# Square sums of the queries as four plain float32 matmuls in array strips, in a cross-attention and FFN kernel

## The reference

```python
q = (layernorm(x) @ Wq).reshape(B, Sq, H, D)      # 16 x 100 tokens, H = 16 heads, D = 128
k = (ctx @ Wk).reshape(B, Skv, H, D)              # 361 context rows of width 256 for each sequence
q = q * rsqrt(mean(q * q, over D) + 1e-5) * gq    # the same for k with gk
attn = softmax(q . k / sqrt(D))
x = x + (attn @ v) @ Wo
x = x + ffn(layernorm(x))                          # 512 -> 4096 gate and up, gelu(gate) * up -> 512
```

## Time and profile before

| | us |
|---|---|
| median of three runs | 1963.61 (1963.55 to 1963.71) |
| the profiled execution | 1964.14 |
| its span | 1962.3 |
| busy PE / DVE / POOL / ACT in the span | 1942.6 / 1598.0 / 1139.9 / 1008.1 |

### The profile page before, as it was taken

One profiled execution on the slowest core, in us unless ns is written; L12 is line 12 of the kernel. 1 busy time (PEld: TensorE's weight loads), 2 busy tenths in 40 slices (PEclk: granted clock), 3 DMA queues, 4 the chain that ended last, 5 costly groups with the idle time before them and its releaser, 6 DMA issues.

```text
span 1962.3 us, 33608 instructions
## 1 busy us (share of the span) xinstructions
PE 1942.6 (99%) x11232; PEld 1852.5 (94%) x11232; DVE 1598.0 (81%) x2995; ACT 1008.1 (51%) x2338; POOL 1139.9 (58%) x1272
## 2 busy tenths in 40 slices
PE   8999999999999999999999999999999999999999
PEld 7899899999999999999999999998999999999999
DVE  8878887787887787887778887888888888888875
ACT  5655555555555555555555553444444444444442
POOL 7765665423434333444333335888888888878871
PEclk9999999999999999999999999999999999999999
DMA  6444443423333334333233333211111111111101
GB/s 201 146 130 159 148 150 108 140 92 100 127 110 96 124 101 121 97 118 120 93 95 116 114 102 108 66 33 44 33 33 33 33 33 33 33 33 33 33 1 68
DMA packets 93515, 174.54 MB, mean 89 GB/s; under 512 B 13265, under 2 KB 49761, under 8 KB 91297
## 3 DMA queue, kind: packets, MB, share of 16 engines
q1 hardware_dynamic: 93344, 172.39, 27.6%
HBM read 139.00 MB, written 33.36 MB: 88 GB/s over the span
## 4 chain that ended last, share of the span: by engine, by line
PE 91%; DVE 4%; issue 2%; POOL 2%; ACT 1%; DMA 0%; SPq 0%; DVEq 0%; ACTq 0%; POOLq 0%
PE psum L429 46%; PE psum L820 19%; PE psum L460 6%; PE psum L493 4%; PE psum L517 4%; PE psum L523 3%; PE psum L518 3%; PE psum L502 3%; PE psum L592 1%; PE psum L533 1%; DVE g L1510 0%; DMA xb<-in_x 0%; DVE work L1382 0%; PE psum L538 0%; DVE ysum L1543 0%
## 5 line engine op out<-in xcount | busy, mean ns | idle before, releaser
L928 ACT ACTIVATE work<-psum,stats,q_rstd 100x361 f32<-100x361 f32 x256 | 163.8, 650 | 166.8 <-DVE stats L1373 166.8
L1272 DVE TENSOR_TENSOR kaT_lo<-psum,kaT_hi 128x488 fp32r<-128x488 f32 (+2 forms) x384 | 213.7, 612 | 38.5 <-ACT kaT_hi L868 38.4
L429 PE MATMUL psum<-wk,ctxT_hi 128*122 128x512 f32 x768 | 241.0, 395 | 0.0
L2044 POOL TENSOR_TENSOR inter_lo<-g,inter_hi 128x400 fp32r<-128x400 f32 x127 | 143.1, 1131 | 126.1 <-ACT inter_hi L868 125.3
L868 ACT CAST kaT_hi<-psum 128x488 fp32r<-128x488 f32 (+2 forms) x384 | 178.7, 540 | 48.7 <-PE psum L502 48.7
L1888 POOL TENSOR_TENSOR k_ss<-k_ss,power 122x4 f32<-122x4 f32 x192 | 193.9, 1010 | 16.0
L1886 POOL TENSOR_SCALAR k_ss<-k_ss 122x4 f32<-122x4 f32 x192 | 37.0, 193 | 260.1 <-DVE k_ss L1328 259.8
L429 PE MATMUL psum<-inter_hi,down_hi 128*128 128x400 f32 x512 | 176.0, 344 | 2.6 <-DVE ysum L1543 1.2
L1363 DVE TENSOR_REDUCE stats<-psum 100x2 f32<-100x722 f32 x128 | 115.6, 903 | 76.1 <-PE psum L460 76.1
L429 PE MATMUL psum<-inter_lo,down_hi 128*128 128x400 f32 x512 | 175.5, 343 | 0.0
L429 PE MATMUL psum<-inter_hi,down_lo 128*128 128x400 f32 x512 | 175.3, 342 | 0.0
(11 more groups left out here) (274 smaller groups left out, 6144.8 us busy)
## 6 DMA issues: line engine op xcount, KB each, us to landing
head_w<-spill_sq SPq DMA_DIRECT2D x48, 512.0 KB, 3.6
head_w<-spill_so SPq DMA_DIRECT2D x46, 512.0 KB, 3.8
wk<-spill_sk SPq DMA_DIRECT2D x12, 1024.0 KB, 4.9
wv<-spill_sv SPq DMA_DIRECT2D x48, 256.0 KB, 2.8
spill_so<-head_w SPq DMA_DIRECT2D x16, 512.0 KB, 3.0
spill_sq<-head_w SPq DMA_DIRECT2D x14, 512.0 KB, 3.0
wk_raw<-in_ctxT SPq DMA_DIRECT2D x12, 361.0 KB, 4.1
spill_sk<-wk SPq DMA_DIRECT2D x4, 1024.0 KB, 6.1
```

The lines of the kernel that those rows point to most:

```text
L429: last = e.matmul(out, a_, b_, start=begins and i == 0, stop=ends and i == len(passes) - 1)
L928: e.activation(attn[h][:, 0:SKV], bank[3 + h][0:SQ, 0:SKV], ACT.Exp, bias=st[:, h:h + 1], scale=rq[:, i * QH + h:i * QH + h + 1], accum_ou ...
L1272: e.tensor_tensor(dst, src, high.bitcast(F32), ALU.subtract).then_inc(S[sem], 1)
L2044: e.tensor_tensor(il[:, :], gact[n % 3][:, :], ih[:, :].bitcast(F32), ALU.subtract).then_inc(S["il"], 1)
```

## The change

From quad 1 on the squares are no longer split. ACT writes the squares of head h to a tile of its own, `q_sq[h]`; the high part (ACT) and the low part (POOL) of the squares are gone, with the waits for them, and so are POOL's waits on `qsh`. TensorE takes four products, one for each head, with operands of type plain float32: the loaded operand is `strip`, 128x32 of ones, the moving one the 128x400 squares, and head h writes rows 32h to 32h+31 of bank 3 (32 equal rows). ACT copies all 128 rows. `sums_transposed` becomes four plain float32 products: the loaded operand is 128x100 of `q_sums`, the moving one the 128x4 `select`, whose column h now picks row 32h. `select` and `strip` are built by six POOL instructions in place of two. Before it writes a square, ACT waits, from quad 2 on, for the four products of the quad before (`qsum` >= quad - 1) in place of `qsl`.

```diff
@@ -55,6 +55,7 @@
 HELD = 3
 TAIL = 4 * STEPS - 8 + 8 * PAIRS - HELD
 WARM = 28
+STRIP = P // QH
 GELU_C = 0.7978845608028654
 GELU_A = 0.044715
 CODE = 2.0 ** -14
@@ -225,8 +226,7 @@
             first_T, first_N, first_sq = [None] * GB, [None] * GB, []
             xlnT = pair(a, "xlnT", [P, DC, GT])
             qT = [[pair(a, f"qT0{h}", [P, GT]) for h in range(QH)]]
-            q_sq = tensor(a, "q_sq", [P, GT])
-            q_sqs = [pair(a, "q_sqs0", [P, GT])]
+            q_sq = [tensor(a, f"q_sq{h}", [P, GT]) for h in range(QH)]
             with ExitStack() as first:
                 first_T[3] = tensor(first, "first_T3", [P, CC * SKV])
                 first_sq += [tensor(first, f"first_sq{h}", [P, GT]) for h in range(2)]
@@ -258,12 +258,12 @@
                     first_N[b] = tensor(first, f"first_N{b}", [KP, KT * CDIM])
             oT = [pair(a, f"oT{i}", [P, GT]) for i in range(QH)]
             xb = [tensor(a, f"xb{i}", [SQ, DIM]) for i in range(GB)]
-            select = tensor(a, "select", [P, QH * QH], F32R)
+            select = tensor(a, "select", [P, QH])
+            strip = tensor(a, "strip", [P, STRIP])
             with ExitStack() as first:
                 own_raw = {n: tensor(first, f"own_raw{n}", [P, DIM]) for n in OWN}
                 own_head = {n: halves(first, f"own_head{n}", DIM) for n in OWN}
-            q_sqs += [pair(a, f"q_sqs{h}", [P, GT]) for h in range(1, QH)]
-            q_sums = tensor(a, "q_sums", [QH, GT])
+            q_sums = tensor(a, "q_sums", [P, GT])
 
         khat = work[:, :].rearrange("p (t n) -> p t n", t=KT)
         attn = [work[0:SQ, h * KPAD:(h + 1) * KPAD] for h in range(QH)]
@@ -394,7 +394,7 @@
         def squares(quad, h):
             if quad == 0:
                 return first_sq[h][:, :], [t[:, :] for t in first_sqs[h]]
-            return q_sq[:, :], [t[:, :] for t in q_sqs[h]]
+            return q_sq[h][:, :], None
 
         def by_head(i, n):
             return bank[i][:, 0:QH * n].rearrange("p (h n) -> p h n", h=QH)
@@ -584,19 +584,16 @@
                 last.then_inc(S["qss"], 1)
 
             def all_squares_summed(quad):
-                e.wait_ge(S["selected"], 2)
+                e.wait_ge(S["selected"], 2 + QH)
+                e.wait_ge(S["qsq"], 4 * quad + QH)
                 for h in range(QH):
-                    e.wait_ge(S["qsh"], 4 * quad + h + 1)
-                    e.wait_ge(S["qsl"], 4 * quad + h + 1)
-                    for k in range(2):
-                        last = e.matmul(bank[3][0:QH, 0:GT], select[:, cols(h, QH)], squares(quad, h)[1][k],
-                                        start=h == 0 and k == 0, stop=h == QH - 1 and k == 1)
+                    last = e.matmul(bank[3][cols(h, STRIP), 0:GT], strip[:, :], squares(quad, h)[0], start=True, stop=True)
                 last.then_inc(S["qsum"], 1)
 
             def sums_transposed(quad):
                 e.wait_ge(S["qsev"], quad)
                 for i in range(GB):
-                    last = e.transpose(bank[7][0:SQ, GT + QH * i:GT + QH * (i + 1)], q_sums[:, cols(i, SQ)], ident[0:QH, 0:QH])
+                    last = e.matmul(bank[7][0:SQ, GT + QH * i:GT + QH * (i + 1)], q_sums[:, cols(i, SQ)], select[:, :], start=True, stop=True)
                 last.then_inc(S["qst"], 1)
 
             def value_of(quad, h, into):
@@ -888,8 +885,8 @@
                 n = 4 * quad + h
                 src = bank[into][:, 0:GT]
                 e.wait_ge(S["q"], n + 1)
-                if n > QH:
-                    e.wait_ge(S["qsl"], n)
+                if quad > 1:
+                    e.wait_ge(S["qsum"], quad - 1)
                 sq, sqs = squares(quad, h)
                 e.activation(sq, src, ACT.Square).then_inc(S["qsq"], 1)
                 if n == 0:
@@ -897,12 +894,9 @@
                 if quad > 1:
                     e.wait_ge(S["sc"], GB * QH * (quad - 1))
                 e.activation(qT[quad % 2][h][0][:, :], src, ACT.Copy, scale=gqk[:, 2:3]).then_inc(S["qTh"], 1)
-                e.wait_ge(S["qsq"], n + 1)
-                if quad > 1:
-                    e.wait_ge(S["qsum"], quad - 1)
-                elif n == QH + 1:
-                    e.wait_ge(S["d_he"], 16 * len(OWN))
-                hi(sqs[0], sq, "qsh")
+                if quad == 0:
+                    e.wait_ge(S["qsq"], n + 1)
+                    hi(sqs[0], sq, "qsh")
 
             def head_hi(h):
                 raw, landed, count = head_source(h)
@@ -1102,7 +1096,7 @@
                     norm2_copy(norm2_at(u - 1), 6)
                 if i == 3 and more:
                     e.wait_ge(S["qsum"], quad + 1)
-                    e.copy(q_sums[:, :], bank[3][0:QH, 0:GT]).then_inc(S["qsev"], 1)
+                    e.copy(q_sums[:, :], bank[3][:, 0:GT]).then_inc(S["qsev"], 1)
 
             u = UNITS - 1
             square(0)
@@ -1901,10 +1895,6 @@
             def query_squares_lo(quad, h):
                 n = 4 * quad + h
                 e.wait_ge(S["qsh"], n + 1)
-                if quad > 1:
-                    e.wait_ge(S["qsum"], quad - 1)
-                elif n == QH:
-                    e.wait_ge(S["qsl"], QH)
                 sq, sqs = squares(quad, h)
                 e.tensor_tensor(sqs[1], sq, sqs[0].bitcast(F32), ALU.subtract).then_inc(S["qsl"], 1)
 
@@ -2075,9 +2065,11 @@
             split_ctx("N", 0)
             query_rstd(0, 2)
             query_rstd(0, 3)
-            e.tensor_scalar(select[:, :], zero[:, :], 1.0, 1.0, ALU.mult, ALU.mult).then_inc(S["selected"], 1)
-            e.wait_ge(S["selected"], 1)
-            e.tensor_scalar(select[:, 0:QH * QH:QH + 1], zero[:, 0:QH], 1.0, 1.0, ALU.mult, ALU.add).then_inc(S["selected"], 1)
+            e.memset(strip[:, :], 1.0).then_inc(S["selected"], 1)
+            e.memset(select[:, :], 0.0).then_inc(S["selected"], 1)
+            e.wait_ge(S["selected"], 2)
+            for h in range(QH):
+                e.tensor_copy(select[:, h:h + 1], ident[:, h * STRIP:h * STRIP + 1]).then_inc(S["selected"], 1)
 
             for u in range(UNITS):
                 quad, i = u // GB, u % GB
@@ -2088,8 +2080,6 @@
                     query_rstds(quad)
                 for n in early_splits(u):
                     split_head(n)
-                if i in (1, 2) and more or u == 3:
-                    query_squares_lo(quad + 1, i - 1)
                 if u + 1 < UNITS:
                     for t in range(KT):
                         key_rstd(u + 1, t)
@@ -2097,8 +2087,6 @@
                     split_ctx("T", 2)
                 if g + 1 < NG and v in (10, 11):
                     ln_rstd(1, coming + 2 * (v - 10))
-                if i >= 2 and more and u != 2 and not (i == 2 and late_splits(u)):
-                    query_squares_lo(quad + 1, i)
                 if norm2_at(u) is not None:
                     ln_rstd(2, norm2_at(u))
                 if g + 1 < NG and v == 11:
@@ -2110,8 +2098,6 @@
                         if g + 1 < NG and v == 10:
                             ln_rstd(1, coming + 1)
                     split_head(n)
-                if i == 2 and u != 2 and late_splits(u):
-                    query_squares_lo(quad + 1, 2)
                 if g + 1 < NG and v == 10 and not late_splits(u):
                     ln_rstd(1, coming + 1)
                 for n in value_splits(u):
```

## The result

The changed kernel takes 1960.65 us (median of 20 runs, 1960.16 to 1963.12); the kernel before, in 20 runs beside it, 1964.07 us. The ratio is 0.9983, 95% interval [0.9977, 0.9989]: 3.4 us or 0.17% faster, clear of noise but inside the 0.2% that the forecast called no change. The profiled execution took 1961.66 us, span 1959.9. It shows less of the gain than the medians do: its first scores stand at 30.2 us against 29.0 before, behind a stretch at the lower of the two clock levels (granted clock 0.50 from 15 to 18 us) that the profile of before doesn't have. Both profiles have one more such stretch of 3.4 us, near 1300 us, in the part that the change doesn't touch.

What follows compares the result with a forecast made beforehand. TensorE's instructions were taken as the bound: -4.8 us on TensorE, -0.5 relief and +0.2 POOL stall sum to -5.1 us, 1959.0 for the profiled execution, 1958.5 us as median. The range was 1950 to 1996 us.

Steps and rivals of the forecast that it cites:

- The bound: From 80 to 1100 us TensorE hardly waits, so the change is priced as TensorE instructions out against instructions in.
- The strips run at once: The four square products of a quad, in different strips, overlap fully, 0.74 us in all; chance 0.40.
- the slower rival: Square products run one after another: 3.66 us a quad with the sums, +28.5 us, so 1992; chance 0.28.
- Squares, 0.74 us for four passes: A plain float32 square product takes four passes of 0.185 us; with 0.08 for strips, 0.82 against 1.48 a quad.
- going in or out of a narrow product costs 0 to 0.08 us now: Boundary cost of the square products, read from steps around the old narrow products; 0.08 us a quad taken.
- the upper bound that stood beside it: A product ends before the next starts at the strips' edges: 0.16 us each side, 0.33 in all.
- The turn, +0.34: Turned sums: four plain products, high and low part each loaded once, 0.62 us, +0.34 us a quad.
- Together: TensorE sum of squares and turn against the old work: -0.32 us a quad, times 15, -4.8 us.
- Relief of ACT and POOL, -0.5: Casts and subtractions removed are covered by TensorE, except near the end of quad 0: -0.5 us, between 0 and -2.
- POOL ahead of its loop, +0.2: Six small POOL instructions for two add 1.2 us; 1.1 us of cover leaves +0.2 us of stall, once.
- Waits: ACT's last square, its 128-row copy, its new `qsum` wait and DVE's variance lose TensorE nothing.
- The staircase: Each square product is two instructions in strict order, only neighbours overlapping: 2.55 us a quad, +12 us, 1975; chance 0.18.

Runs made afterwards that it cites:

- sums_f32r: Changed kernel with copied sums and selection in float32r, so each turn product is one record and sums are rounded once more: 1955.70 us.
- full_turn: Changed kernel with sums turned in all fifteen quads by four float32 transposes against the 128x128 identity into bank 4, two waits added: 1963.92 us.
- one_strip: Changed kernel with all four square products of a quad writing rows 0 to 31 of bank 3: 1989.64 us.
- old_load: Changed kernel with ACT's high parts and POOL's low parts of the squares written again, into unused spare tiles: 1961.53 us.

## Why the prediction was right or wrong

**The bound** was right. In every run that added or took TensorE time without a new wait, the time followed it nearly in full (sums_f32r: 5.0 of 5.3 us), and 85 us of ACT and POOL time were worth 0.9. In full_turn a new wait took more back than the 4.0 us that its turn saved.

**The strips run at once**: right, and this decided the sign; one_strip shows the slower rival's world at 1989.6, near its 1992. The forecast wasn't sure of it: it gave this case 0.40, and slower results 0.52 together. And the 0.17% that came lies in what it called no change, with 0.20.

**Squares, 0.74 us for four passes**: right in kind, 0.67 measured, because the rate is 0.84 ns a column for each of two halves. "So going in or out of a narrow product costs 0 to 0.08 us now ... I take 0.08" **is the step that failed**. It was read off a 4-column float32r product, and not even there is it a price: 0.03 + 0.26 us to the second product is what a transpose and a pass take anyway. In and out of strips costs 0.33 us, in number the upper bound that stood beside it. Squares with their surroundings went down by 0.47 us a quad, not 0.66.

**The turn, +0.34**: two loads a product, 0.088 us each, was right for its records. The net was +0.25, since the old 4-row turn, as its steps read, carried a cost of its own that the forecast did not see; this took back part of the miss on the squares.

**Together** the group of squares, output products and turn takes 4.15 us instead of 4.39 in quad 4, from the last key transpose to the second score product. (The output products between are 0.02 us shorter.) Summed over the 15 quads, of 0.19 to 0.24 each, it is -3.4 us against -4.8.

**Relief of ACT and POOL, -0.5**: it was more, and the forecast misread its rows. It put most of the 0.9 us that TensorE idled from 75 to 90 us down to the copy of the sums. In the trace of the kernel before, that wait stands behind 90 us, and this is all that TensorE waited for from 75 to 90 us:

```profile
PE psum L502 <- DVE work L1382: 0.9, 2, 0.6
```

The attention transposes got 0.61 us shorter there (unit 3) and 0.37 us in unit 11, which the forecast didn't look at; old_load gives 0.61 and 0.35 of it back. They also got 0.28 us shorter in unit 2, which old_load does not give back; its cause was not followed up. **POOL ahead of its loop, +0.2**: the small instructions took 0.86 us in place of 0.46, +0.4 and not +1.2, and unit 0 is still 15.12 us long; worth nothing. (The split behind them ends at 37.29 us, but in a profile whose first scores came 1.2 us later.) **Waits**: the copy, the variance and ACT's new wait cost nothing new, as said.

Added up piece by piece from the first scores on, the trace has -3.7 us: -3.4 in the groups, -1.3 at the attention transposes of units 2, 3 and 11, and +1.0 that comes back. Of this, 0.3 stands at the attention transposes of units 4, 8 and 12; the rest is in steps of a few hundredths of a us and was not followed up. So that the groups make just the 3.4 us by which the medians differ is partly luck: the relief and the unexplained loss nearly cancel. Against 1958.5 us the time is off by 2.2, 0.5 of which is that the kernel before had a median of 1963.61 in three runs and 1964.07 in twenty.

**The staircase** gave two instructions for a product, and that was so. The order was not: the first halves of all four strips start before the second half of any. Whether the chip or the instruction stream orders them so was not tested.

## What to carry to other kernels

Small products in plain float32 with 32 loaded columns each ran side by side here when they wrote different strips, but the group pays a fixed way in and out (0.33 us here): worth it from about two passes saved, and worth more the more strip work stands in one group. Read a group's price from the last instruction ahead of it to the second one behind it, since its boundary cost stands in the neighbours' pieces. When a result is turned on TensorE, count loads and not columns (here four loads with 128 columns took 0.44 us, eight loads with 4 columns 0.62), and put it where the next writer of that bank comes late: the same transposes lost 3.3 us against the changed kernel with one bank (15 quads) and won 2.1 with another (7 quads).

## What the runs showed that I had not expected

- A plain float32 product is two loads and two matmuls of 336 ns at 400 columns, and in four strips the first halves start 7 ns apart, the second halves 340 ns after the last first half.
- Strips cost 0.33 us a group in and out, and one strip alone costs nearly the same; plain float32 with all 128 columns costs nothing at its ends.
- A turn with 4-row operands costs 0.26 us a group more than a 128-row one with the same number of records.
- A wait two score products behind its producer cost up to 1.2 us in a unit and 7.3 us in all fifteen, while the profile's wait rows sum to 3.3 us. The loss was seen only by comparing units.
- A relief of ACT and POOL that looks like one place was two: the second, in unit 11, was seen only by comparing units.
